# Last tile's reciprocal roots by a power operation on GpSimd, shared with VectorE and ScalarE by stream; value sums ahead of projections once all scores are out

## What is computed

```python
x = x + layernorm(attention(layernorm(x)))     # 16 heads of 16 channels, causal, with a projection
x = x + layernorm(ffn(layernorm(x)))
# attention: softmax(q k^T / 4) v over 4096 keys, then the projection w_proj (+ its low-rank part)
# ffn: three blocks of
#   y = layernorm(h @ W0.T + b0) * gamma + beta
#   h = h + gelu(y) @ W1.T + b1
# layernorm: (x - mean) / sqrt(var + 1e-5), over the 256 channels of a row
```

## Time and profile before

| | us |
|---|---|
| median of 3 runs | 1272.06 (1270.0 to 1274.13) |
| the profiled execution's own time | 1270.7 |
| its span in the trace | 1269.0 |
| PE busy in the span | 1214.9 (96%) |
| ACT busy | 1103.6 (87%) |
| DVE busy | 764.6 (60%) |
| POOL busy | 439.3 (35%) |

### The profile page before, as it was taken

One profiled execution on the slowest core, in us unless ns is written; L12 is line 12 of the kernel. 1 busy time (PEld: TensorE's weight loads), 2 busy tenths in 40 slices (PEclk: granted clock), 3 DMA queues, 4 the chain that ended last, 5 costly groups with the idle time before them and its releaser, 6 DMA issues.

```text
span 1269.0 us, 30124 instructions
## 1 busy us (share of the span) xinstructions
PE 1214.9 (96%) x11429; PEld 526.0 (41%) x11429; DVE 764.6 (60%) x1867; ACT 1103.6 (87%) x1263; POOL 439.3 (35%) x1397
## 2 busy tenths in 40 slices
PE   8999999999999999999999999999999999999866
PEld 6556434343343434434433343333334333342255
DVE  6775226567755765786565775765766564640076
ACT  4665999999999999999999998999899999999633
POOL 3221235433433553355234344342233422220053
PEclk9999999999999999999999999999899999999979
DMA  5985644645434544444444244453434343320000
GB/s 173 317 303 176 185 121 127 189 142 144 127 117 122 154 112 124 125 121 144 122 132 133 78 139 116 113 144 90 126 117 129 112 125 96 103 85 24 5 1 17
DMA packets 144208, 159.48 MB, mean 126 GB/s; under 512 B 76326, under 2 KB 106044, under 8 KB 144060
## 3 DMA queue, kind: packets, MB, share of 16 engines
q1 hardware_dynamic: 139772, 153.26, 40.9%
q10 hardware_dynamic: 4288, 4.26, 1.1%
HBM read 117.62 MB, written 35.65 MB: 121 GB/s over the span
## 4 chain that ended last, share of the span: by engine, by line
PE 68%; ACT 7%; DVE 6%; issue 3%; DMA 3%; POOL 2%; SPq 2%; ACTq 0%; DVEq 0%
PE O L1496 30%; PE S L1478 21%; PE F L209 15%; ACT probs L1421 6%; SPq L595 1%; DMA feed_mem<-turns 1%; DMA qkv_mem<-turns 1%; PE S L1567 1%; DVE stC L1590 1%; DVE feed_mem L1697 0%; DVE o_turned L1646 0%; DVE tmpC L1607 0%; DVE feed_mem L1714 0%; DVE feed_mem L1698 0%; PE S L1565 0%
## 5 line engine op out<-in xcount | busy, mean ns | idle before, releaser
L1421 ACT ACTIVATE probs<-S 128x1024 f32<-128x1024 f32 x1056 | 995.3, 1050 | 65.2 <-PE S L1478 56.3
L1496 PE MATMUL O<-probs,vg 128*32 128x512 f32 (+3 forms) x4608 | 524.3, 565 | 4.7 <-DVE o_turned L1646 3.8
L1478 PE MATMUL S<-q_op,k_op 64*128 64x512 f32 (+3 forms) x2304 | 384.4, 425 | 9.6 <-ACT probs L1421 7.6
L1478 PEld LDWEIGHTS S<-q_op,k_op 64*128 64x128 f32 x2304 | 186.5, 184 | 324.3 <-ACT probs L1421 235.1
L1496 PEld LDWEIGHTS O<-probs,vg 128*32 128x32 f32 x4608 | 120.4, 109 | 207.9 <-issue 178.8
L1399 POOL TENSOR_SCALAR_AFFINE_SELECT probs<-probs 128x512 f32<-128x512 f32 (+1 forms) x160 | 92.1, 585 | 165.1 <-ACT probs L1421 164.5
L1372 POOL TENSOR_SCALAR tmpC<-mvC 128x2 f32<-128x2 f32 x84 | 25.7, 306 | 310.0 <-DVE rstdC L1599 308.2
L209 PE MATMUL F<-wfT,feed_mem 128*32 128x256 f32 x1280 | 81.8, 382 | 3.5 <-DMA feed_mem<-turns 1.9
L1646 DVE STREAM_TRANSPOSE o_turned<-O 128x512 f32<-128x512 f32 x32 | 22.8, 712 | 100.6 <-PE O L1496 99.6
L1698 DVE SCALAR_TENSOR_TENSOR feed_mem<-feed_mem 128x512 f32<-128x512 f32 x90 | 66.3, 737 | 3.1
L1697 DVE SCALAR_TENSOR_TENSOR feed_mem<-feed_mem 128x512 f32<-128x512 f32 x90 | 63.5, 706 | 3.5 <-DVE qkv_mem L1703 0.5
(11 more groups left out here) (207 smaller groups left out, 1288.4 us busy)
## 6 DMA issues: line engine op xcount, KB each, us to landing
k_op<-qk_rows SPq DMA_DIRECT2D x256, 256.0 KB, 3.6
qk_rows<-parts SPq DMA_DIRECT2D x32, 512.0 KB, 4.6
q_op<-qk_rows SPq DMA_DIRECT2D x128, 128.0 KB, 2.9
turns<-feed_mem SPq DMA_DIRECT2D x160, 64.0 KB, 1.9
feed_mem<-turns SPq DMA_DIRECT2D x40, 256.0 KB, 2.9
k_op<-qk_rows SPq DMA_DIRECT2D x48, 128.0 KB, 2.6
x_in<-in_L_attn_x ACTq DMA_DIRECT2D x8, 512.0 KB, 5.1
feed_mem<-in_L_attn_x SPq DMA_DIRECT2D x16, 256.0 KB, 3.4
```

The costliest lines, as they stand in the source:

```text
L1421: nc.scalar.activation(probs[:, n % NP, :, :], S[:, n % NS, :, :], ACT.Exp, scale=SCALE).then_inc(exp_ok, 1)
L1478: last = nc.tensor.matmul(S[:, n % NS, a, at:at + TT - q0], k_op[mine, c % RING, pair, k0:k0 + P], q_op[mine, v % QS, pair, q0:TT], start= ...
L1496: last = nc.tensor.matmul(O[h * STRIP:(h + 1) * STRIP, q0:TT], vg[:, kb, col:col + STRIP], probs[:, n % NP, a, at:at + TT - q0], start=fir ...
```

## The change

Three things.

1. Roots of tile 7. `moments` no longer makes a guess: it writes variance + eps to `rstd` and minus half of it to `tmp`, two instructions with no wait between them. POOL then raises `rstd` to the power -0.5 in one instruction (`tensor_tensor` with a column of -0.5, `minus_half`). For streams 1 and 3 POOL goes on with one Newton step and `nmr`, and ACT applies them as before. For streams 0 and 2 POOL does the power alone; DVE takes one Newton step (`refine`) and then applies (value - mean) * `rstd` to the 256 channels itself. So `rs` of streams 0 and 2 moves from DVE to POOL, and `norm`/`sc` of streams 0 and 2 from ACT to DVE.
2. Value sums have rank -1 once all scores are out.
3. The times that `plan()` books for these steps are new, and with them the order in the tail.

```diff
-    if t == NT - 1 and name.startswith(("norm", "copy", "sc")):
+    if t == NT - 1 and (name.startswith("copy") or k % 2 and name.startswith(("norm", "sc"))):
         return "ACT"
-    if t == NT - 1 and k % 2 and (name.startswith("rs") or name in ("add_x", "result")):
+    if t == NT - 1 and (name.startswith("rs") or k % 2 and name in ("add_x", "result")):
         return "POOL"
...
-                time = (SQUARE_POOL if name.startswith("sq") else ROOT_POOL if t < NT - 1 else 2.0 if name.startswith("rs") else 0.8) if eng == "POOL" else short if t == NT - 1 else time
+                time = (SQUARE_POOL if name.startswith("sq") else ROOT_POOL if t < NT - 1 else (1.5 if k % 2 else 0.6) if name.startswith("rs") else 0.8) if eng == "POOL" else 0.9 if t == NT - 1 and eng == "DVE" and name.startswith(("norm", "sc")) else short if t == NT - 1 else time
...
             if x[0] == "weigh":
-                return 0.5 if backlog >= BACKLOG else 2
+                return -1 if scores == NUNIT else 0.5 if backlog >= BACKLOG else 2
...
+        minus_half = sb("minus_half", [P, 1])
...
-                    for n in range(3):
-                        link(s, nc.gpsimd.tensor_scalar(w, r, r, v, ALU.mult, ALU.mult))
-                        link(s, nc.gpsimd.tensor_scalar(r, w, 1.5, r, ALU.add, ALU.mult))
+                    power = nc.gpsimd.tensor_tensor(r, r, minus_half[:, :], ALU.pow)
+                    if k % 2 == 0:
+                        return power
+                    link(s, power)
+                    link(s, nc.gpsimd.tensor_scalar(w, r, r, v, ALU.mult, ALU.mult))
+                    link(s, nc.gpsimd.tensor_scalar(r, w, 1.5, r, ALU.add, ALU.mult))
                     return nc.gpsimd.tensor_scalar(nmr[:, b], mv[:, b, 0], -1.0, r, ALU.mult, ALU.mult)
...
                     if t == NT - 1:
-                        link(s, nc.vector.tensor_scalar(tmp[:, 1, b], mv[:, b, 1], -0.5, -0.5 * EPS, ALU.mult, ALU.add))
-                        return nc.vector.tensor_scalar(rstd[:, b].bitcast(I32), tmp[:, 1, b].bitcast(I32), -0.5, HALVED_SEED, ALU.mult, ALU.add)
+                        nc.vector.tensor_scalar(tmp[:, 1, b], mv[:, b, 1], -0.5, -0.5 * EPS, ALU.mult, ALU.add)
+                        return nc.vector.tensor_scalar(rstd[:, b], mv[:, b, 1], EPS, None, ALU.add)
...
-                    if t == NT - 1:
-                        r, w, v = rstd[:, b], tmp[:, 0, b], tmp[:, 1, b]
-                        for n in range(3):
-                            link(s, nc.vector.tensor_scalar(w, r, r, v, ALU.mult, ALU.mult))
-                            link(s, nc.vector.tensor_scalar(r, w, 1.5, r, ALU.add, ALU.mult))
-                        return nc.vector.tensor_scalar(nmr[:, b], mv[:, b, 0], -1.0, r, ALU.mult, ALU.mult)
...
+                def refine(s, b):
+                    r, w, v = rstd[:, b], tmp[:, 0, b], tmp[:, 1, b]
+                    link(s, nc.vector.tensor_scalar(w, r, r, v, ALU.mult, ALU.mult))
+                    link(s, nc.vector.tensor_scalar(r, w, 1.5, r, ALU.add, ALU.mult))
...
+                link(0, nc.vector.memset(minus_half[:, :], -0.5))
...
+                    elif t == NT - 1 and name.startswith(("norm", "sc")):
+                        if name == "sc_att":
+                            stored_before(dve, t, k)
+                        b = slots(t, k)
+                        refine(s, b)
+                        nc.vector.tensor_scalar(own(y, t, k)[:, 0, :], (xt if name == "norm_x" else normed(name, t, k))[:, 0, :], mv[:, b, 0], rstd[:, b],
+                                                ALU.subtract, ALU.mult).then_inc(dve_ok[s], 1)
```

## The result

The changed kernel takes 1260.96 us (median of 6 runs, 1260.12 to 1263.82) against 1271.03 us for the kernel before (6 runs beside them): 10.1 us less, a ratio of 0.9919 with a 95% interval of 0.9903 to 0.9935, which is 8 to 12 us. The prediction was 8.8 us.

The account below looks back on a forecast made before the run. It took a 73 us tail of short dependent DVE and POOL instructions, partly with PE at half clock, as the bound. 2.8 + 0.5 + 3.0 - 0.8 + 3.0 + 0.7 + 0.2 - 0.6 = 8.8 gave 1263.2 us, range 1260 to 1265.5.

Parts of the forecast that it names:

- value sum first: Start of the tail: the last value sum no longer waits behind six project products, bringing later steps 2.8 us earlier.
- clock in the last projections: Last four projections: PE may keep full clock instead of half, saving between 0 and 0.6 us, taken as 0.5.
- att and x: Normalizations att and x: shorter roots on POOL, which sets this stretch, save 3.0 us together.
- block 0 up to `gelu0` 1: From `turn_x` 1 to `gelu0` 1: more products ahead of `turn0` 1, partly at half clock, lose 0.8 us.
- blocks on DVE: Blocks 0, 1 and 2: less root work on DVE saves 1.5 us each in 1 and 2, 0.7 in 0.
- the end: From `ln_h` 1 on: DVE's gain is eaten by a new wait on POOL, leaving 0.2 us.
- contention: Tail: POOL instructions slowed beside DVE adds with two SBUF operands, 0.6 us taken off.
- The power's price: One power on POOL, shown in no row: taken as 0.5 us, range 0.2 to 2.7.
- A slow power (1 and 2): Powers on POOL: at 0.9 us, gain 5.2 (chance 0.17); at 1.7 us, kernel 8 us slower (chance 0.11).
- A first call that pays (3): First power, in att: one stall of 5 to 8.8 us, time 1268.2 to 1272; 0.13 shared with two other cases.
- Only the reordering pays (4): Tail: only the moved value sum gains, roots nothing net, time 1269.6 us; chance 0.13 shared with two other cases.
- The clock (5): Block 0: PE longer at half clock loses 1.5 us, full clock wins 2; 1261 to 1264.7, no separate chance.

Follow-up runs that it names:

- e3: The changed kernel with each of the 24 powers done twice on POOL, first into a scratch column; median 1271.1 us.
- e1: The kernel before with only the value sums ranked first once all scores are out; median 1269.1 us.
- e7: The changed kernel with 32 idle PE products behind the last projection; median 1267.7 us.
- e11: The changed kernel with 14 idle PE products behind the last projection; median 1261.5 us.
- e13: The changed kernel with old roots in streams 0 and 2 and old booked times, so lists as with only the value sum moved; median 1265.4 us.
- e6: The changed kernel with a one-column Gelu on ACT right after the last exponential, loading the table early; median 1259.3 us.
- e9: The changed kernel with the early Gelu, 32 idle PE products, and stream 0's last power ahead of the add of result 3; median 1262.5 us.
- e10: The changed kernel with the early Gelu, 14 idle PE products, and stream 0's last power ahead of the add of result 3; median 1256.59 us.
- e12: The changed kernel with the early Gelu and stream 0's last power ahead of the add of result 3, no idle products; median 1259.6 us.
- e4: The changed kernel with the old roots of streams 0 and 2 (DVE, then ACT), the power in streams 1 and 3 only; median 1268.0 us.
- e5: The changed kernel with the whole root of all four streams on POOL and the application on ACT; median 1266.2 us.

## Why the prediction was right, step by step

The measured lengths in the two profiles, against the terms of the sum.

| term | predicted | measured | from |
|---|---|---|---|
| value sum first | 2.8 | 2.78 | start of the turn of `O` at 3.92, then 1.14 |
| clock in the last projections | 0.5 | 0.52 | from there to `ln_att`: 6.42, then 5.90 |
| att and x | 3.0 | 3.12 | to `turn_x` 1: 12.30, then 9.18 |
| block 0 up to `gelu0` 1 | -0.8 | -1.16 | 9.27, then 10.43 |
| blocks on DVE | 3.7 | 4.43 | to `ln_h` 1: 28.34, then 23.91 |
| the end | 0.2 | 0.05 | 12.90, then 12.85 |
| contention | -0.6 | in the others | |
| sum | 8.8 | 9.74 | |

**The power's price** was a guess between 0.2 and 2.7 and held: 0.5 against 0.554. No row of the trace before had it, and how POOL computes a power no run shows, so that it came out so near is luck; it is the number on which the whole forecast stood, and e3 shows that twice the price would have brought nothing.

**The clock in the last projections** came out at 0.5 in the two profiles, and in e1 at 0.2: with the value sum first the clock fell 6.3 to 6.9 us after the release in e1, e7, e11 and e13, and not before 11 us in the eight other kernels that have it first. The term was rightly called open.

**Att and x** took POOL and DVE together. From `ln_att` to `turn_x` 1 it is 12.30 in e1, 11.06 in e13, where POOL's roots alone are shorter, and 9.18 in the changed kernel. I wrote that POOL sets this stretch; DVE's roots stood right behind.

**Block 0** came out near, -1.16 for -0.8, by two errors that cancel. The start of `turn0` 1 was put 9.4 us after that of `turn_x` 1 (the products, 4.5 us of them at half clock, and the waits), and came after 8.40, with PE at half clock for 3.1 us. Behind it I had 0.7 for `turn0` 1 and its drain up to `gelu0` 1, and it was 2.03: ACT stood at `norm0` 3, whose root waits in POOL's list, and then loaded its table. In the kernel before the load was there too, right behind the last copy:

```profile
1226.24 0.44 PE L1547 MATMUL S<-ident,feed_mem 128*128 128x128 f32 x2
...
1226.46 1.28 ACT L1436 ACT_TABLE_LOAD   x1
```

`turn0` 1 ran beside it, and it was 1.52 us from there to `gelu0` 1. So about half of the 1.16 is PE's, as I had it (8.40 us where it was 7.75), and half is the place of the load (2.03 where it was 1.52). e6 prices the load at 1.56 us. The clock, which was in my sum, costs 1.0 to 1.2 there (e9 and e10 against e6, e11 against the changed kernel); the load was not in the sum, although it was in the rows of ACT that I had before me.

**The blocks.** The 1.5 each for blocks 1 and 2 is what DVE saved in them: from the moments of stream 0 to what follows the roots 1.59 and 1.44. In block 2 DVE needs 4.28 us from the moments of stream 0 to what follows the roots, where the earlier trace rows had 5.72 and I had 4.1:

```profile
1242.37 0.43 DVE L1594 BATCH_NORM_STATS2 stC<-F 128x6 f32<-128x256 f32 x1 [0.40 <-PE F L1571]
...
1246.65 0.43 DVE L1594 BATCH_NORM_STATS2 stC<-S 128x6 f32<-128x256 f32 x1
```

The 0.7 that came on top of 3.7 lies elsewhere. In block 0, where I had 0.7, it is 0.95 (from `gelu0` 1 to `ln1` 0 10.01 before and 9.06 after), and another 0.45, for which I had no term, lies between `add1` 1 and `ln2` 0. DVE's application from PSUM took 0.54 and not the 0.41 of a row whose source is SBUF, but the next instruction starts 0.45 after it.

**The end** is as read from the list: the power of stream 0 behind the adds of streams 1 and 3, DVE idle for 1.49 us, and the gain on DVE eaten. Its swap is worth 0.69 us (e9).

**Contention** was rated a little too high. It shows twice:

```profile
1211.89 0.75 DVE L1731 TENSOR_TENSOR feed_mem<-feed_mem 128x256 f32<-128x256 f32 x2
1212.24 0.62 POOL L1389 TENSOR_SCALAR tmpC<-rstdC,tmpC 128x1 f32<-128x1 f32 x1
...
1255.02 0.66 POOL L1385 TENSOR_TENSOR rstdC<-rstdC,minus_half 128x1 f32<-128x1 f32 x1 [2.02 <-DVE rstdC L1601]
```

A Newton instruction took 0.28 us more beside DVE's two adds, and the last power 0.11 more beside one: 0.4 us together, against the 0.6 that I took off. That is what the Trainium skill's page GPSIMD Engine Reference (Key points) says of DVE instructions with two SBUF inputs, and it struck only beside those.

**The rivals.** A slow power (1 and 2): not met, but my slope was too small. I counted nine powers on the path; e3 shows 13 to 16, so that no gain is left at some 1.2 us and not at 1.37. A first call that pays (3): the first power took 0.57 us, like the rest; the 6 us for a freshly loaded routine, which the Trainium skill's page GPSIMD Engine Reference names under Instruction dispatch, don't appear here. Only the reordering pays (4): e1 against the changed kernel, 3.2 of 9.7. The clock (5): inside the range, as forecast. A clock at full speed from `turn_x` 1 on would have been worth 1.0 to 1.2 us up to `gelu0` 1, and a second fall costs 1.6, which the rival did not have.

## What to carry to other kernels

When a chain of short instructions on two engines is shortened, shorten both: the power in the streams of one engine alone gave 1.6 us of tail, and with the other engine's roots taken away too, under new lists, it gave 6.6. Read each engine's in-order list for what has come to stand ahead of a wait, table loads and queued adds among it; here two entries in the wrong place were worth 2.3 us one by one and 1.6 together (e12). A list scheduler's booked times are part of the change: with one set of them 1.6 us of gain became 0.6 of loss (e4, e13), a part of it perhaps by the clock. And before two profiled executions are subtracted, compare the granted clock stretch by stretch: a fall in one of them was worth 1.6 us here, as much as most of the steps.

## What the runs showed of the hardware that I had not expected

- A power of one column on POOL takes 0.554 us (24 of them), next to 0.27 to 0.37 for the Newton instructions there, and the first is no slower. Two in a row, with a wait between them, start 0.62 to 0.74 us apart (e3).
- Two small DVE instructions with no wait between them start 0.07 us apart, where a linked pair starts 0.19 apart: the moments went from four linked instructions to 0.81 us from one stream to the next.
- Ahead of `second0` the granted clock fell to half in six of the seven kernels in which PE had waited 1.46 or 1.68 us for ACT, from 0.2 us before PE went back to work (e5) to 1.1 us after (e11), and stayed there for some 3.4 us; in none of the seven with a wait of 0.99 us or less. Moving the table load into an idle stretch of ACT (e6, e9, e10, e12) took that wait away.
- Products that no one reads were in e7, e9, e10 and e11. In e9 and e10 the granted clock stayed at 1.00 and that paid 1.0 to 1.1 us up to `gelu0` 1; the whole kernel was faster for it once the stretch was short enough to end before the next real product was due (e10); in e7 and e11 it fell before them, behind the wait for the DMA, and again behind the table load.
